# A decoder layer on one core: gate and up weights stationary, streamed for each expert job, rows weighed before the experts

## The reference, cut to what matters

```python
xn = _layernorm(x, ln_gamma, ln_beta)
...
probs = e / (jnp.sum(e, axis=-1, keepdims=True) + ROUTER_EPS)
...
topk_p, topk_i = jax.lax.top_k(probs, TOP_K)
dense_gate = jnp.zeros((N, N_EXPERTS), probs.dtype).at[jnp.arange(N)[:, None], topk_i].add(topk_p)
for eid in range(N_EXPERTS):
    xe = xf * dense_gate[:, eid:eid + 1]
    gu = xe @ gate_up_w[eid].T
    gate, up = jnp.split(gu, 2, axis=-1)
    hidden = jax.nn.silu(gate) * up
    out = out + hidden @ down_w[eid].T
return x + out.reshape(B, S, D)
```

## Time and profile before

| | |
|---|---|
| median of 3 runs | 285.28 us (284.24 to 286.21) |
| span of the profiled execution | 285.3 us |
| TensorE, VectorE, ScalarE, GpSimd busy | 240.7, 185.4, 163.6, 127.3 us |
| attention stage | to about 185 us |
| expert jobs | about 185 to 272 us |
| final loads, sums and stores | from 267.6 us to the end |

### The profile page before, as it was taken

The page is one execution under the profiler, slowest core; times in us unless marked ns, Lnnn a source line. Parts: engine busy times, 40 slices in busy tenths (PEclk is TensorE's granted clock), DMA queues, the critical chain, the costliest instruction groups (busy, mean ns, idle before and its releaser), DMA issues.

```text
span 285.3 us, 9260 instructions
## 1 busy us (share of the span) xinstructions
PE 240.7 (84%) x3122; PEld 175.4 (61%) x3122; DVE 185.4 (65%) x822; ACT 163.6 (57%) x347; POOL 127.3 (45%) x184
## 2 busy tenths in 40 slices
PE   6859999989998999989989695688869899999800
PEld 2748787878777777867858564444446566666500
DVE  2636687889888888877976966646533454444443
ACT  2443786677667657757857524368434466677500
POOL 1032321432374574575264547353734475555530
PEclk9997999999999999999999977559968999999965
DMA  7997999200000000000000000211211222232366
GB/s 236 244 409 292 368 410 407 105 3 2 2 22 14 12 31 3 12 31 9 12 27 13 21 20 22 56 50 43 74 49 47 75 74 68 71 79 66 97 187 188
DMA packets 19054, 28.17 MB, mean 99 GB/s; under 512 B 3118, under 2 KB 13617, under 8 KB 18624
## 3 DMA queue, kind: packets, MB, share of 16 engines
...
q10 hardware_dynamic: 1296, 1.46, 1.7%
...
## 4 chain that ended last, share of the span: by engine, by line
PE 45%; issue 20%; DVE 10%; POOL 9%; SPq 4%; DMA 4%; ACT 3%; another core or an unknown queue 2%; DVEq 1%; POOLq 0%
PE six L478 33%; PE few_bank L478 4%; POOL rstd L1918 3%; POOL slots L1975 3%; DMA ctx_all<-in_ctx 3%; PE six L569 2%; PE six L822 2%; DMA y_all<-results 2%; PE six L802 1%; POOL vcb L1935 1%; POOL rstd_a L1918 1%; PE turn_bank L478 1%; SPq L378 1%; SPq L405 1%
## 5 line engine op out<-in xcount | busy, mean ns | idle before, releaser
L1918 POOL TENSOR_TENSOR rstd<-var,cst 128x1 f32<-128x1 f32 (+1 forms) x32 | 25.3, 791 | 84.1 <-DVE var L1278 54.7
L2016 POOL DMA_INDIRECT results<-y_sb,meta x39 | 38.1, 977 | 34.4 <-issue 19.9
L478 PE MATMUL six<-guT_sb,gT_sb 128*128 x78 | 44.0, 650 | 0.3
L1975 POOL DMA_INDIRECT slots<-pay,slot_i x32 | 32.8, 1024 | 12.0 <-issue 7.6
L1660 DVE TENSOR_TENSOR hid<-jsilu,six 128x256 f32<-128x256 f32 x39 | 16.3, 419 | 24.9 <-ACT jsilu L1060 24.0
L478 PE MATMUL six<-downT_sb,hT_sb 128*128 x156 | 26.1, 292 | 4.9 <-DVE y_sb L1676 3.8
L1060 ACT ACTIVATE jsilu<-six,g_sb 128x256 f32<-128x256 f32 x39 | 18.5, 474 | 17.3 <-PE six L478 15.7
L478 PEld LDWEIGHTS six<-downT_sb,hT_sb 128*128 128x128 f32 x156 | 22.0, 201 | 10.1 <-issue 9.9
L1071 ACT ACTIVATE gT_sb<-six,small_sb 128x128 f32<-128x128 f32 x39 | 17.8, 458 | 9.8 <-PE six L802 8.9
L1003 ACT ACTIVATE etanh<-six,xscale 128x1024 f32<-128x1024 f32 x16 | 17.8, 1114 | 8.9 <-PE six L478 8.9
L1676 DVE TENSOR_SCALAR y_sb<-six,meta 128x128 f32<-128x128 f32 x39 | 13.5, 347 | 13.5 <-PE six L478 9.1
...
## 6 DMA issues: line engine op xcount, KB each, us to landing
...
```

The costliest lines, as they stand in the source:

```text
L478: return pe.matmul(o, lhsT=l, rhs=r, start=start, stop=stop, **kw)
L1918: nc.gpsimd.tensor_tensor(dst, src, half[:, 0:dst.shape[1]], ALU.pow).then_inc(semaphore, 1)
L1975: nc.gpsimd.indirect_dma_start(slots, bass.IndirectOffsetOnAxis(slot_i[k][:, c:c + 1], 0), pay[k][:, c // TOPK, c % TOPK, :], None, bounds ...
L2016: nc.gpsimd.indirect_dma_start(results, bass.IndirectOffsetOnAxis(meta[k][:, 1:2].bitcast(I32), 0), y_sb[k][:, :], None, bounds_check=TOPK ...
```

## The change

Each job's gate and up weights (256 KB) are now loaded for it by SyncE into `gu_sb`, a ring of 6, behind its `g_sb` load; `guT_sb` is gone. The weights are the stationary operand in four pieces of 128 columns, `gT_sb` moves. So the result is transposed already, Silu and product make `hidT` directly, and `turn_h` is gone from TensorE and ScalarE. Since a row is now a column there, its probability can't be a per-partition scale any more: the rows are weighed when they are filled in (`fill_rows`), and gamma and beta are applied on VectorE ahead of that, from `norm_w`, which is spread over partitions once. `xhat` is made on GpSimd. PSUM for gate and up has four buffers in place of three; the tables hold slot and expert of a job side by side.

```diff
-        guT_sb = sb("guT_sb", [P, E, 2 * F])
...
+        norm_w = sb("norm_w", [P, 2, D])
+        xc_sb = several("xc_sb", [P, D])
...
+        gu_sb = [sb(f"gu_sb{k}", [P, 2 * F]) for k in range(RING)]
         g_sb = [sb(f"g_sb{k}", [P, ROW]) for k in range(RING)]
         gT_sb = [sb(f"gT_sb{k}", [P, P]) for k in range(3)]
-        jsilu = [sb(f"jsilu{k}", [P, F]) for k in range(3)]
-        hid = [sb(f"hid{k}", [P, F]) for k in range(3)]
-        hT_sb = [sb(f"hT_sb{k}", [P, 2, P]) for k in range(3)]
-        meta = [sb(f"meta{k}", [P, 2]) for k in range(RING)]
+        jsilu = [sb(f"jsilu{k}", [P, F]) for k in range(4)]
+        hidT = [sb(f"hidT{k}", [P, F]) for k in range(4)]
+        meta = [sb(f"meta{k}", [P, 1]) for k in range(RING)]
         y_sb = [sb(f"y_sb{k}", [P, D]) for k in range(RING)]
-        gu_ps = [sw_bank, quad[:, 0], quad[:, 1]]
+        gu_ps = [sw_bank, quad[:, 0], quad[:, 1], quad[:, 3]]
         gT_ps = ko_bank[:, 0:P]
-        hT_ps = quad[:, 3, 0:F]
...
-            for dst, src, done in ((ctxT_all, ctxT, l_ctxT), (guT_sb, guT, l_gu),
+            for dst, src, done in ((ctxT_all, ctxT, l_ctxT),
...
-                after(sp, jsilu_ready, j - RING)
                 after(sp, g_turned, j - RING)
                 settle(sp)
-                where = early[0:1, j:j + 1] if j < EARLY else table[0:1, j - EARLY:j - EARLY + 1]
-                r = nc.values_load(
+                where = early[0:1, 2 * j:2 * j + 2] if j < EARLY else table[0:1, 2 * (j - EARLY):2 * (j - EARLY) + 2]
+                _, (r, x) = nc.values_load_multi_w_load_instructions(
                     where, engines=[mybir.EngineType.SP], min_val=0, max_val=SLOTS - P,
                     skip_runtime_bounds_check_because="a job of an expert starts within its "
                     "region, and of the others there are at most SPARE")
+                x = nc.s_assert_within(
+                    x, 0, E - 1, skip_runtime_bounds_check_because="made on the chip as min(sum of flags, E - 1)")
                 sp.dma_start(g_sb[k][:, :], slots[bass.ds(r, P), :]).then_inc(l_job[k], 16)
+                after(sp, gu_done, j - RING)
+                sp.dma_start(gu_sb[k][:, :], guT[:, bass.ds(x, 1), :].rearrange("p a f -> p (a f)")
+                             ).then_inc(l_gu[k], 16)
...
+            def spread_norm():
+
+                pe.wait_ge(l_c, 16)
+                pe.wait_ge(l_small, 16)
+                for n in range(2):
+                    ins = mm(few_bank[:, n * D:(n + 1) * D], vecs[:, n + 1:n + 2].broadcast_to([P, P]),
+                             ident)
+                ins.then_inc(norm_done, 1)
...
             def gate_up(j):
                 if j == 0:
-                    pe.wait_ge(l_gu, 16)
                     after(pe, x1_ready, NT - 1)
-                elif j < 3:
+                elif j < 4:
                     after(pe, tanh_ready, NT - 1)
                 else:
-                    after(pe, hid_ready, j - 3)
+                    after(pe, hid_ready, j - 4)
                 after(pe, gT_ready, j)
-                mm(gu_ps[j % 3], gT_sb[j % 3][:, :], at(guT_sb, experts[j])).then_inc(gu_done, 1)
-
-            def turn_h(j):
-                if j == 0:
-                    after(pe, tanh_ready, NT - 1)
-                after(pe, hT_ready, j - 1)
-                after(pe, hid_ready, j)
-                for f in range(2):
-                    ins = pe.transpose(hT_ps[:, f * P:(f + 1) * P],
-                                       hid[j % 3][:, f * P:(f + 1) * P], ident)
-                ins.then_inc(h_turned, 1)
+                pe.wait_ge(l_gu[j % RING], 16 * (j // RING + 1))
+                for f in range(4):
+                    ins = mm(gu_ps[j % 4][:, f * P:(f + 1) * P],
+                             gu_sb[j % RING][:, f * P:(f + 1) * P], gT_sb[j % 3][:, :])
+                ins.then_inc(gu_done, 1)
 
             def down(j):
                 if j == 0:
                     pe.wait_ge(l_down, 16)
                     after(pe, a_ready, NT - 1)
                 after(pe, y_ready, j - 1)
-                after(pe, hT_ready, j)
+                after(pe, hid_ready, j)
                 e = experts.pop(j)
                 for f in range(2):
-                    ins = mm(y_ps, hT_sb[j % 3][:, f, :],
+                    ins = mm(y_ps, hidT[j % 4][:, f * P:(f + 1) * P],
                              downT_sb[:, bass.ds(e, 1), f, :].rearrange("p a d -> p (a d)"),
                              start=(f == 0), stop=(f == 1))
                 ins.then_inc(y_done, 1)
...
             route(15)
             gate_up(2)
-            turn_h(0)
-            turn_h(1)
             turn_g(4)
             down(0)
             gate_up(3)
...
                 if i < JOBS:
                     gate_up(i)
-                if i - 1 < JOBS:
-                    turn_h(i - 1)
                 down(i - 2)
...
             def turn_xn(t):
                 after(act, xn_turned, t)
-                nc.scalar.activation(xnT_sb[t % BUFS], tr_ps, ACT.Identity, bias=vecs[:, 2:3],
-                                     scale=vecs[:, 1:2]).then_inc(xnT_ready, 1)
+                copy(xnT_sb[t % BUFS], tr_ps).then_inc(xnT_ready, 1)
+
+            def keep_norm():
+                act.wait_ge(norm_done, 1)
+                copy(norm_w[:, :, :].rearrange("p n d -> p (n d)"),
+                     few_bank[:, 0:2 * D]).then_inc(norm_ready, 1)
...
             def gate(j):
                 after(act, gu_done, j)
-                nc.scalar.activation(jsilu[j % 3][:, :], gu_ps[j % 3][:, 0:F], ACT.Silu,
-                                     scale=g_sb[j % RING][:, D:D + 1]).then_inc(jsilu_ready, 1)
-
-            def turn_h(j):
-                after(act, h_turned, j)
-                after(act, y_done, j - 3)
-                copy(hT_sb[j % 3][:, :, :].rearrange("p f t -> p (f t)"), hT_ps).then_inc(hT_ready, 1)
+                nc.scalar.activation(jsilu[j % 4][:, :], gu_ps[j % 4][:, 0:F],
+                                     ACT.Silu).then_inc(jsilu_ready, 1)
 
             def turn_g(j):
                 after(act, g_turned, j)
                 after(act, gu_done, j - 3)
-                nc.scalar.activation(gT_sb[j % 3][:, :], gT_ps, ACT.Identity, bias=vecs[:, 2:3],
-                                     scale=vecs[:, 1:2]).then_inc(gT_ready, 1)
+                copy(gT_sb[j % 3][:, :], gT_ps).then_inc(gT_ready, 1)
 
             evacuate_k(15)
...
-            for i in range(FULL, JOBS + 1):
+
+            for i in range(FULL, JOBS):
                 if i + 1 < JOBS:
                     turn_g(i + 1)
-                if i < JOBS:
-                    gate(i)
-                turn_h(i - 1)
+                gate(i)
...
+            def center_x(t):
+
+                if t == 0:
+                    dve.wait_ge(norm_ready, 1)
+                after(dve, x2_mean, t)
+                nc.vector.scalar_tensor_tensor(
+                    out=xc_sb[t % BUFS], in0=x2_sb[t % ROWS], scalar=mv2[t % BUFS][:, 0:1],
+                    in1=norm_w[:, 0], op0=ALU.subtract, op1=ALU.mult).then_inc(xc_ready, 1)
+
             def norm_x(t):
+                after(dve, xc_ready, t)
                 after(dve, x2_rstd, t)
                 after(dve, pay_ready, t - ROWS)
-                nc.vector.tensor_scalar(xn_sb[t % ROWS], x2_sb[t % ROWS], mv2[t % BUFS][:, 0:1], rstd2[t % BUFS][:, 1:2],
-                                        ALU.subtract, ALU.mult).then_inc(xn_ready, 1)
-
-            def norm_xhat(t):
-                nc.vector.tensor_scalar(xhat[t % ROWS], x2_sb[t % ROWS], mv2[t % BUFS][:, 0:1], rstd2[t % BUFS][:, 0:1],
-                                        ALU.subtract, ALU.mult).then_inc(xhat_ready, 1)
+                nc.vector.scalar_tensor_tensor(
+                    out=xn_sb[t % ROWS], in0=xc_sb[t % BUFS], scalar=rstd2[t % BUFS][:, 1:2],
+                    in1=norm_w[:, 1], op0=ALU.mult, op1=ALU.add).then_inc(xn_ready, 1)
...
-                nc.vector.tensor_copy(pay[k][:, :, :, D], top[:, :, :])
...
             def gate(j):
                 after(dve, jsilu_ready, j)
-                after(dve, h_turned, j - 3)
-                nc.vector.tensor_tensor(hid[j % 3][:, :], jsilu[j % 3][:, :], gu_ps[j % 3][:, F:2 * F],
+                after(dve, y_done, j - 4)
+                nc.vector.tensor_tensor(hidT[j % 4][:, :], jsilu[j % 4][:, :], gu_ps[j % 4][:, F:2 * F],
                                         ALU.mult).then_inc(hid_ready, 1)
...
-                nc.vector.tensor_copy(meta[k][:, :], g_sb[k][:, D:D + 2]).then_inc(meta_ready, 1)
-
-            def scale(j):
+                nc.vector.tensor_copy(meta[k][:, :], g_sb[k][:, D + 1:D + 2]).then_inc(meta_ready, 1)
+
+            def take_y(j):
                 k = j % RING
                 after(dve, y_done, j)
-                after(dve, meta_ready, j)
                 if j >= RING:
                     dve.wait_ge(y_out[k], 16 * (j // RING))
```

(16 more changed lines are left out.)

133 lines of the change are left out of this document (59 added, 74 removed).

## The result

The changed kernel takes 298.86 us (median of 4 runs, 296.24 to 301.15), the kernel before 284.76 on the same chip: ratio 1.0495, 95% interval 1.0427 to 1.0563. The forecast was 282.6, its range 276.5 to 287.5.

What follows compares the result with a forecast made beforehand. The prediction took TensorE to bound attention and a two-job chain of 3.41 us (1.71 a job) the expert stage. Terms: 285.3 - 0.5 (loop) - 2.4 (ahead of job 15) + 0.2 (center_x) = 282.6 us, range 276.5 to 287.5.

Steps and rivals of the forecast that it cites:

- No matmul there changes, so this stage stays.: Attention stage: TensorE is busy 18.70 of 20 us and its matmuls are unchanged, so no time changes there.
- "Nothing" for GpSimd's work: GpSimd's added xhat and weighed fill, under 11 us in all, fit into its waiting for VectorE and cost nothing.
- Ahead of job 15: Expert jobs before job 15: removed transposes of hid let queued TensorE work move up, -2.4 us, bounds 0 and -3.5.
- `center_x` +0.2: VectorE in the last tiles: center_x replaces xhat ahead of the choosing steps and xn, costing 0.2 us once.
- The loop: Expert stage's two-job chain, gate-up to y to next gate-up: 3.41 becomes 3.36 us, -0.5 us over 18 jobs.
- Rivals two: Expert stage: the loop isn't the limit; pace follows TensorE's work, some 1.50 us a job, total 279.3; chance 0.12.
- five: Gate-up in the expert stage: eight weight loads are exposed, 0.6 us more a job, total 293; chance 0.03.
- Equal to the median of the runs: Whole kernel: the profiled span of 285.3 us equals the runs' median, so the sum needs no correction.
- The stream: SyncE's per-job weight loads: issue some 1.25 us a job, landing in time five jobs ahead, cost nothing.
- rival four: Expert stage: weights come late and gate-up waits for them, +0.27 us a job, total 289.5; chance 0.12.
- Rival three: Idle engines at 206 to 208 us and the half clock after it disappear, -5.6 us, total 277.0; chance 0.20.

Runs made afterwards that it cites:

- e13: Changed kernel with carry (xhat and sum on GpSimd) moved behind the two scatters of a tile step; 288.51 us, ratio 1.0175.
- e2: Only the weights' half of the change on the kernel before: streamed stationary weights, no turn_h, rows not weighed, xhat on VectorE; 284.25 us, ratio 0.9933.
- e14: e2 with expert 0's weights loaded for every job, so SyncE loads one register word instead of two; 283.76 us, ratio 0.9990.
- e1: Only the rows' half of the change on the kernel before: rows weighed, xhat on GpSimd, weights resident, turn_h kept; 298.86 us, ratio 1.0492.
- e6: Changed kernel with a pair's third scatter one tile later and the last three carries between the last pair's scatters; 290.89 us, ratio 1.0182.

## Why the prediction was wrong, point by point

- **"No matmul there changes, so this stage stays."** This is the step that failed, and with it 9.0 of the 10 us between the two profiles. The bound of a stage was read from TensorE's own instructions; what counts as well is which of GpSimd's DMAs run beside them. The text itself had named a change of this stage's pace as what would prove it wrong.
- **"Nothing" for GpSimd's work, hidden in 54.7 us of waiting.** Two errors. The mis-sized term: `xhat` takes 0.80 us, not "near" 0.45; the weighed fill 0.62 instead of 0.41. The wrong reasoning: idle time of an engine hides work only if what stands behind it has slack. Behind `carry` stand the scatters (e13 shows the price: the ratio falls from 1.0495 to 1.0175, some nine of the 14 us), and behind the last three `carry` the sends. For these the text allowed 1.5 us and found it harmless, "keep_meta asks for it six jobs later"; it waited 2.94 us.
- **The price of `xhat`.** The rows show 0.80 us for `xhat` on GpSimd; before, at 105.19, VectorE took 0.34 for the same operation. The Trainium skill, "GPSIMD Engine Reference", section Engine selection, calls one-input operations roughly line-rate there and two-input ones about twice as slow. Here the one-input form with two scalars is the slow one (2.3 times), the two-input sum takes 0.46; the measurement decides.
- **Ahead of job 15, -2.4, and `center_x` +0.2.** The number is near, -1.6 to the y of job 13, but that isn't shown to be its mechanism: the weights' half alone, which holds the whole term, takes 48.1 us (e2) and 49.2 (e14) over this stretch against 48.7 before, and after has standstills there that before has not. As far as the runs go, luck.
- **The loop, -0.03 a job.** The pace is right: -0.02. The working is not borne out in detail. The distance from y to the next load was called constant from three rows (1.05, 1.06, 1.06); in the same trace it lies between 0.98 and 1.15 from 229 to 264, and in after it is 0.94 and 1.19 at two turns in a row. Gate-up to y is 2.21. Rivals two (a job of 1.5) and five (exposed loads) are out: a job takes 1.68, and the eight records of gate-up from 256.81 to 257.94, 1.13 us. Each half alone is quicker than both together, 1.62 (e2) and 1.65 (e1); why stays open.
- **"Equal to the median of the runs."** The span of 285.3 was, but a span is 1.8 us less than its execution's time, so the sum was made against an execution slower than the median. That moves the forecast by under 2 us and explains little of the miss.
- **The stream, nothing.** Right in effect, mis-sized in SyncE's share (1.57 for 1.25). `gu_sb` is never a last wait: rival four is out.
- **Rival three, the standstill goes.** Out: a wait of 2 us or more on remote stays in every version but e6, which has the 3.62 on issue; after has several (y at 214.87 waits 2.53 us, at 219.30 2.94 us, both on remote, beside six indirect DMAs in a row). That it sits where indirect DMAs follow each other was to be seen beside the earlier trace rows, and would have been the hint for the whole case: four scatters and a send in a row from 201.6 to 207.7, and three engines idle at 206 to 208.
- **Missing altogether**: a rival in which the change shifts a stage that it doesn't touch. The one on the slower side was a bandwidth story.
